# A selective scan on one core: all sixteen diagonals of B by way of DRAM, one state a transfer, and both parts of the step made by ScalarE

## The reference

```python
x_dbl = einsum('bkdl,kcd->bkcl', xs, x_proj_w)      # 40 rows: 8 of dt, 16 of B, 16 of C
delta = softplus(einsum('bkrl,kdr->bkdl', dts, dt_proj_w) + dt_proj_b)
def step(h, inp):                                   # h: (b, k, d, n)
    dA = exp(dt[..., None] * A4)
    h = dA * h + (dt * ut)[..., None] * bt[:, :, None, :]
    y = einsum('bkdn,bkn->bkd', h, ct)
```

## Time and profile before

| | |
|---|---|
| median of 3 runs | 6563.44 us (6556.88 to 6565.86) |
| profiled execution | 6549.5 us, span 6547.8 us |
| TensorE busy | 5769.2 us (88%) |
| VectorE busy | 4636.9 us (71%) |
| ScalarE busy | 3051.9 us (47%) |
| GpSimd busy | 2737.6 us (42%) |
| mean granted TensorE clock | 0.953 |
| DMA | 858.30 MB, mean 131 GB/s |

### The profile page before, as it was taken

The page is one execution under the profiler, slowest core; times in us unless marked ns, Lnnn a source line. Parts: engine busy times, 40 slices in busy tenths (PEclk is TensorE's granted clock), DMA queues, the critical chain, the costliest instruction groups (busy, mean ns, idle before and its releaser), DMA issues. The chain is left out here.

```text
span 6547.8 us, 128900 instructions
## 1 busy us (share of the span) xinstructions
PE 5769.2 (88%) x41691; PEld 5133.7 (78%) x41691; DVE 4636.9 (71%) x6690; ACT 3051.9 (47%) x5802; POOL 2737.6 (42%) x1648
## 2 busy tenths in 40 slices
PE   7799999999778999999997527999999979999998
PEld 5688888888657888888885415888888878888887
DVE  2799999999618999999995653556555565555554
ACT  2688888888537887888884211111111111111110
POOL 1688898889518898988893000000000000000000
PEclk8899999999889999999998868999999989999999
DMA  2455555554414555554542135666666666667665
GB/s 92 108 136 137 135 138 134 137 136 136 124 58 121 135 137 133 140 133 131 136 135 88 32 82 144 146 149 154 151 151 138 147 163 145 142 145 149 152 150 142
DMA packets 1081548, 858.30 MB, mean 131 GB/s; under 512 B 304598, under 2 KB 987446, under 8 KB 1046966
## 3 DMA queue, kind: packets, MB, share of 16 engines
q1 hardware_dynamic: 1080566, 844.65, 52.5%
q10 hardware_dynamic: 720, 10.49, 0.4%
HBM read 811.44 MB, written 43.55 MB: 131 GB/s over the span
## 5 line engine op out<-in xcount | busy, mean ns | idle before, releaser
L714 POOL TENSOR_TENSOR read<-state,c_wide 128x1024 f32<-128x1024 f32 x1024 | 2420.4, 2380 | 367.6 <-DVE state L763 361.3
L763 DVE TENSOR_TENSOR_SCAN state<-decay,carry,p_drive 128x512 f32<-128x512 f32 x1792 | 2152.8, 1260 | 53.8 <-POOL carry L718 24.8
L648 ACT ACTIVATE decay<-step,a_neg 128x512 f32<-128x512 f32 x2048 | 1422.2, 717 | 419.4 <-DVE state L763 405.3
L1646 PE MATMUL p_y<-window,x_high 128*128 128x256 f32 x7936 | 1497.4, 286 | 0.0
L1709 ACT COPY term_blocks<-p_s 128x256 f32<-128x256 f32 x832 | 310.4, 373 | 2184.8 <-PE p_s L1646 2184.8
L1646 PEld LDWEIGHTS p_y<-window,x_high 128*128 128x128 f32 x7936 | 1246.1, 191 | 0.0
L1646 PE MATMUL p_y<-window,x_low 128*128 128x256 f32 x3968 | 1134.2, 286 | 0.0
L542 PE MATMUL p_drive<-diag_b,xu_tok 128*128 128x128 f32 x8192 | 1068.4, 284 | 50.1 <-DVE state L763 50.1
L542 PEld LDWEIGHTS p_drive<-diag_b,xu_tok 128*128 128x128 f32 x8192 | 1006.2, 199 | 112.8 <-DVE state L763 107.8
L553 PE MATMUL p_y<-ident,read 128*128 128x128 f32 x8192 | 1077.6, 275 | 9.0 <-POOL read L714 5.9
L553 PEld LDWEIGHTS p_y<-ident,read 128*128 128x128 f32 x8192 | 940.1, 143 | 11.1 <-POOL read L714 11.1
(11 more groups left out here) (245 smaller groups left out, 5358.6 us busy)
## 6 DMA issues: line engine op xcount, KB each, us to landing
c_wide<-c_scratch SPq DMA_DIRECT2D x256, 1024.0 KB, 4.7
diag_b<-diag_scratch SPq DMA_DIRECT2D x256, 512.0 KB, 4.1
window<-taps_scratch SPq DMA_DIRECT2D x448, 257.0 KB, 6.3
window<-taps_scratch SPq DMA_DIRECT2D x768, 129.0 KB, 4.6
window<-taps_scratch SPq DMA_DIRECT2D x192, 513.0 KB, 7.2
window<-taps_scratch SPq DMA_DIRECT2D x64, 385.0 KB, 6.1
gate_scratch<-gate_out SPq DMA_DIRECT2D x16, 512.0 KB, 3.1
gate_in<-gate_scratch SPq DMA_DIRECT2D x8, 1024.0 KB, 6.4
```

Of the source, the lines that this page charges most:

```text
L648: act.activation(decay[:, n % 2, t, :], step[:, c.parity, t, :], ACT.Exp, scale=m.a_neg[:, DT2 * c.k + t, n:n + 1]).then_inc(s["decay"], 1)
L714: pool.tensor_tensor(read[:, n % 4, :, :], state[:, n % 4, :, :], wide, ALU.mult).then_inc(s["read_out"], 1)
L763: dve.tensor_tensor_scan(flip(state[:, n % 4, t, :], c), flip(decay[:, n % 2, t, :], c), flip(p_drive[:, n % 2, t, :], c), 0.0 if c.start ...
L1646: last = pe.matmul(out, x[:, source, blk, :], view[:, :, at:at + P][:, :, ::-1], start=first and x is m.x_high and z == 0, stop=True, skip ...
```

## The change

In the scan:

- every state's diagonal goes by way of DRAM: `store_rows` writes 16 x 512 single values where it wrote 8 x 512, `load_diag` loads one state (256 KB) a transfer into one of four slots, and `drive` is a product for every n. `turn_b`, `keep_b` and `times_b` are gone;
- both step products of a chunk stand at n = 2, in two banks (`p_prep` and `p_b`), and ScalarE makes both parts of the step from them (`step_parts`: |z| and max(z, 0) for each half), then one exponential of 1024 columns and one logarithm. `step_bias` of VectorE is gone;
- `turn_y`, `keep_y`, `add_y` and `keep_x` stand at other n;
- at the start 8 MB of zeros are written, where 4 MB were.

In the spectral layer the window `w` is loaded and waited for in two halves (`w` for slot 16, `v` for slot 18), and `build` is cut into `sum_weights` and `scale_weights` at slots 3 to 6. The attention frees its semaphores and ends with a barrier of all engines.

```diff
             def load_diag(c, n):
-                if not (c.first and d < 2):
-                    sp.wait_ge(s["driven"], START + c.q * 2 + (8 * d - 8))
-                at = 2 * d * NB4 * P * P
-                src = m.diag_dram[c.parity, at:at + 2 * NB4 * P * P].rearrange("(n p q) -> p n q", n=2 * NB4, p=P)
+                if not (c.first and n < 4):
+                    sp.wait_ge(s["driven"], START + c.q * 2 + (2 * n - 6))
+                src = m.diag_dram[c.parity, n * NB4 * P * P:(n + 1) * NB4 * P * P]
...
-                    ap=[[NB4 * P * P, ODD], [P * P, NB4], [P + 1, P]])
-                rows = xd[B_ROW + 1:B_ROW + NS:2, :].rearrange("n (i p) -> n i p", p=P)
+                    ap=[[NB4 * P * P, NS], [P * P, NB4], [P + 1, P]])
+                rows = xd[B_ROW:B_ROW + NS, :].rearrange("n (i p) -> n i p", p=P)
...
             def drive(c, n):
-                if n % 2 == 0:
-                    pe.wait_ge(s["scaled"], START + c.g * ODD + (n // 2 + 1))
-                elif n % 4 == 1:
-                    pe.wait_ge(s[f"diag_in{n // 4 % 2}"], START + c.g * 32 + (16 * (n // 8) + 16))
+                if n == 0:
+                    pe.wait_ge(s["x_kept"], START + c.g * 2 + 2)
+                pe.wait_ge(s[f"diag_in{n % 4}"], START + c.g * 64 + (16 * (n // 4) + 16))
...
-                        if n % 2 == 0:
-                            last = pe.transpose(o, scaled[:, i, t * P:t * P + P], m.ident[:, :])
-                        else:
-                            last = pe.matmul(o, xu_tok[:, c.parity, i, t * P:t * P + P],
-                                             diag[:, n // 4 % 2, n // 2 % 2, i, :], start=True, stop=True)
+                        last = pe.matmul(o, xu_tok[:, c.parity, i, t * P:t * P + P], diag[:, n % 4, i, :],
+                                         start=True, stop=True)
...
+            def step_parts(c):
+                if not c.first:
+                    act.wait_ge(s["decay"], START + c.q * 2 + -2 * NS)
+                act.wait_ge(s["x_turned"], START + c.g * 2)
+                for t in range(DT2):
+                    act.wait_ge(s["step_mm"], START + c.g * 2 + (t + 1))
+                    bias = m.dt_b[:, DT2 * c.k + t:DT2 * c.k + t + 1]
+                    bank = (p_prep, p_b)[t]
+                    act.activation(softplus[:, t, :], bank[:, :], ACT.Abs, bias=bias).then_inc(s["step_abs"], 1)
+                    act.activation(step[:, c.parity, t, :], bank[:, :], ACT.Relu, bias=bias).then_inc(s["step_max"], 1)
...
                 if c.first:
-                    step_bias(c, 0)
-                    step_bias(c, 1)
                     begin_y(0)
                     finish_step(c)
                     begin_y(1)
                 for n in range(NS):
                     scan(c, n, 0)
-                    if n in (6, 7) and not c.first:
-                        add_y(Before(c), n - 6)
-                    if nxt and n in (4, 5):
-                        step_bias(nxt, n - 4)
+                    if n in (7, 9) and not c.first:
+                        add_y(Before(c), n // 2 - 3)
                     if nxt and n == 8:
                         finish_step(nxt)
                     scan(c, n, 1)
...
-    "w": [(1, 256, 256), (1, 512, 512), (5, 128, 512)],
+    "w": [(1, 256, 256), (5, 128, 256)],
+    "v": [(1, 512, 512), (5, 384, 512)],
...
-                        build(n, k, 0)
+                    if i in (3, 5):
+                        sum_weights(n, k, (i - 3) // 2)
+                    if i in (4, 6):
+                        scale_weights(n, k, (i - 4) // 2)
```

More of the change, by code:

```diff
@@ L93, in _ @@
             sp.wait_ge(idmade, 4)
-            for parity in range(2):
-                sp.dma_start(m.diag_dram[parity].rearrange("(r x) -> r x", r=P), blank[:, :]).then_inc(m.w_stored, 16)
+            for part in range(4):
+                half = m.diag_dram[part // 2].rearrange("(h r x) -> h r x", h=2, r=P)[part % 2]
+                sp.dma_start(half, blank[:, :]).then_inc(m.w_stored, 16)
             sp.wait_ge(copied, 14)
@@ L407, in scans @@
         xd = sb("xd", [P, L])
-        b_tok = sb("b_tok", [P, 2, NB4, NS])
         c_wide = sb("c_wide", [P, 2, 4, L])
@@ L561, in turn_y @@
                     pe.wait_ge(s["y_kept"], START + c.g + 1)
-                    pe.wait_ge(s["b_kept"], START + c.g + (1 if c.last else 2))
+                    pe.wait_ge(s["step_max"], START + c.g * 2 + (2 if c.last else 6 if c.following else 4))
                 else:
@@ L571, in body @@
                     project(c)
-                    turn_b(c)
                     step_product(c, 0)
@@ L579, in body @@
                 for n in range(NS):
-                    if not c.first and n in (5, 6):
-                        turn_y(Before(c), n - 5)
+                    if not c.first and n in (6, 7):
+                        turn_y(Before(c), n - 6)
                     if nxt:
@@ L630, in step_ln @@
                 act.activation(softplus[:, :, :], softplus[:, :, :], ACT.Ln, bias=1.0).then_inc(s["step_ln"], 1)
-            def times_b(c, n):
-                if n == 0:
-                    act.wait_ge(s["b_kept"], START + c.g + 1)
-                    act.wait_ge(s["x_kept"], START + c.g * 2 + 2)
-                if not (c.first and n < 2):
-                    act.wait_ge(s["driven"], START + c.q * 2 + (2 * n - 2))
-                for i in range(NB4):
-                    last = act.activation(scaled[:, i, :], xu_tok[:, c.parity, i, :], ACT.Copy,
-                                          scale=b_tok[:, c.parity, i, n:n + 1])
-                last.then_inc(s["scaled"], 1)
             def decays(c, n, t):
@@ L669, in body @@
                     keep_projection(c)
-                    keep_b(c)
+                    step_parts(c)
                     step_exp(c)
@@ L674, in body @@
                     keep_x(c, 1)
-                    times_b(c, 0)
                     for n in range(2):
@@ L678, in body @@
                         decays(c, n, 1)
-                    times_b(c, 2)
                 for n in range(NS):
@@ L683, in body @@
                         decays(of, at, 0)
-                    of, at = following(c, nxt, n + 3)
-                    if of and at % 2 == 0:
-                        times_b(of, at)
                     of, at = following(c, nxt, n + 2)
@@ L689, in body @@
                         decays(of, at, 1)
-                    if n == 3 and not c.first:
+                    if n == 2 and not c.first:
                         keep_y(Before(c))
@@ L807, in __init__ @@
         self.g, self.q, self.first = c.g + -1, c.q + -NS, False
+        self.last, self.following = False, not c.last
         self.last = False
@@ L1174, in _ @@
                                                  ALU.mult, ALU.add).then_inc(s["res"], 1)
+    nc.clear_and_free_semaphores(list(s.values()))
+    nc.all_engine_barrier()
 KF, LAGS, FRACS = 16, 3, 4
@@ L1218, in held_in @@
         return "c"
-    return {0: "near", 1: "w", 3: "x" if g < 8 else "y"}[v]
+    return {0: "near", 1: "w" if g % 2 == 0 else "v", 3: "x" if g < 8 else "y"}[v]
 def columns(name, vector, lag):
-    at = 0
+    at = BEGIN.get(name, 0)
     for v, low, top in RUNS[name]:
@@ L1618, in body @@
                 load("w", k)
+                load("v", k)
                 if following is None:
@@ L1659, in slot @@
                 for j, (v, lag, blk) in enumerate(full):
-                    if i == 16 and v == 1:
-                        pe.wait_ge(s["in_w"], START + n * (32 * len(RUNS["w"])) + 32 * len(RUNS["w"]))
+                    if i in (16, 18) and v == 1:
+                        half = "w" if i == 16 else "v"
+                        pe.wait_ge(s["in_" + half], START + n * 64 + 64)
                     last = product(shared_bank(i), source, DIFF + blk // 2, held_in(g, v), v, lag, j == 0)
```

106 lines of the change are left out of this document (45 added, 61 removed).

## The result

The changed kernel takes 7029.46 us (median of 4 runs, 7019.83 to 7035.25) against 6560.16 us of the kernel before beside it: ratio 1.0714, interval 1.0697 to 1.0731. It is slower, as forecast, but by 469 us where the forecast had 263.

A forecast was written before the change was run, and what follows sets the result against it. VectorE leads before, TensorE after: 48.0 + 3.3 wait + 0.7 clock = 52.0 us a chunk, + 4.85 x 62 = + 301; with - 21 - 22 + 5, + 263 on 6549.5, as median 6826 us; range 6600 to 7050.

The forecast's parts named there:

- The mechanism: Scan: TensorE becomes the bound with 48.0 us of work a chunk and waits before drive 8 for diagonals behind the store.
- VectorE's relief: Scan: VectorE loses 2.9 us a chunk, down to 40.9, worth nothing because TensorE becomes the bound.
- The forecast proper: Whole kernel: waits of 1.5 to 5 us a chunk give 6696 to 6950 us; chance 0.61.
- rival B: Scan: store worse than linear, or clock falling in every chunk; 7167 us, milder half from 6950; chance 0.14.
- The wait: Scan: TensorE waits 3.3 us a chunk before drive 8 for its diagonal, load 8, queued behind the store.
- The store itself: Scan: 8192 single values in SyncE's one queue take 11.5 us, bounds 10 and 16, ending at T + 15.1.
- T: Scan: the end of drive 3, when load 7 and the store may go; TensorE wants drive 8 at T + 13.85.
- with the slower transfers behind a store and the landing T + 17.1: Scan: load 8 ends at T + 15.9, and with slow transfers and landing is there at T + 17.1.
- The clock term: Scan: waits go on provoking half clock on TensorE, taken as 0.7 us a chunk; 1.7 if in every chunk.
- In this regime scans have 3 us of slack: Scan: with TensorE the bound, scans have 3 us to the drive two states later, so VectorE no longer delays TensorE.
- case A: Scan: TensorE bounds but loads are in time, wait 0 to 1.5 us; 6590 to 6696 us; chance 0.17.
- The small terms: Outside the chunk: first chunk of each image -21 us, spectral rounds -22, zeros and barrier at the start + 5.

The follow-up runs named there:

- split_blocks_dve: split_blocks with VectorE making both parts of the step again, as in step_on_dve; 6775.87 us, ratio 1.0323 to the kernel before.
- keep_busy: The changed kernel with 40 transposes of the identity put ahead of drive 8 in each chunk; 6910.34 us, ratio 1.0555 to the kernel before.
- half_rows: The changed kernel storing only the diagonals of states 0 to 7, 4096 values in place of 8192; 6741.06 us, ratio 1.0299 to the kernel before.
- store_act: The changed kernel with both stores issued by ScalarE in its own queue, not SyncE's; 6803.02 us, ratio 1.0395 to the kernel before.
- split_blocks: The changed kernel with the store cut into four between the loads, each 128 places of all sixteen rows; 6726.64 us, ratio 1.0275 to the kernel before.
- step_on_dve: The changed kernel with VectorE making both step parts again and ScalarE's exponential in two halves; 6870.99 us, ratio 1.0496 to the kernel before.
- adjacent_rows: The kernel before, storing the adjacent rows 0 to 7 of B in place of the odd ones; 6567.92 us, ratio 1.0004.

## Why the prediction was right, and where its sizes were off

**The mechanism was right.** TensorE is the bound; it waits once a chunk, before drive 8, for the diagonals behind the store; and the sign follows. VectorE's relief was said to be worth nothing, and that is nearly so: by split_blocks_dve it is worth 31 us (by the ratios) to 49 us (by the medians), while in the changed kernel itself undoing it even wins 158 us. The drive costs 1.79 us for each state (842.42 to 844.21), as forecast, and TensorE's work is 48.8 us by keep_busy against 48.0. half_rows, store_act and split_blocks each take most or all of the wait away in another way and win 226 to 303 us.

**The place in the range owes something to luck.** The forecast proper, waits of 1.5 to 5 us, ended at 6950 us. The measured 7029 us lie above it, in what the range took in of rival B ("the clock falls in every chunk", chance 0.14), 20 us short of the range's end at 7050. That half of B is what happened: the wait stayed under 5 us, and the clock falls behind it in 61 of the 62 chunks that have a store, where the kernel before has it in 32 of 62 (low stretches of the granted clock, counted in the traces).

**The wait was undersized: 4.55 us a chunk, not 3.3.** The store itself was oversized: issued at 832.61, 1.15 us behind the end of drive 3 at T = 831.46, its values are nearly through by 844, T + 12.5, where the working had T + 15.1. But the transfers behind it are slow for six microseconds, where the working allowed about one: load 8 is there at T + 18.8 in place of T + 17.1. Two errors, 2.6 us too much and 4.3 too little, met in one sum, so that the wait came out only 1.3 us short. The working also had SyncE issue load 8 as soon as its slot was free, while that issue is held until 843.3, when the store is nearly through. (One end of the bounds was added up wrongly: a store of 10 us gives T + 3.6 + 10 + 0.8 = T + 14.4 and a wait of 0.5, not 14.1 and 0.3.) The earlier trace rows had shown the slow transfers; the step "with the slower transfers behind a store and the landing T + 17.1" took too little for them.

**The clock term was undersized most: 2.26 us a chunk, not 0.7.** The forecast left half of the falls out, since before the falls came in half of the chunks. With TensorE waiting 4.55 us at the same place in every chunk the clock falls each time, and in the window it is at half for 64.9 us, 5.1 a chunk, where the working had 3.4 for a fall. The Trainium skill ("TensorE: Matmul & The Clock Gate", section "HAM oscillation — how this bites in real kernels") says that a recurring DMA wait in a loop throttles the clock in each pass; the trace agrees, with the 61 of 62 chunks. The 1.7 us that the prediction had for a fall in every chunk was the better number, and still too low.

**VectorE is closer behind than the forecast had it.** "In this regime scans have 3 us of slack" holds in the changed kernel only because TensorE stands still for the diagonals. Where that is gone, in split_blocks, TensorE waits for the scans 17.2 / 13.9 = 1.2 us a chunk by its products alone, up to 3.1 with its weight loads (25.6 + 17.2), and the chunk is 50.22 us. So case A's 6590 to 6696 could not have been reached with the loads in time: the runs put it at 6727. In the changed kernel itself these waits are 0.5 us a chunk, and some 0.2 us remain that the sum had not.

The chunk is then 48.0 + 4.55 + 2.26 + 0.7 = 55.5 us, as measured. The scan of the two images, from the first scan to the last, is longer by 533 us (62 x 8.38 = 520, and 14 in the first and last chunks) where the forecast had 301.

**The small terms were right.** The first image's first scan starts at 210.2 us in place of 222.5, and the second's comes 9.9 us sooner after the last of the first image, together 22.2, as forecast (-21): `begin_y` starts at 181.69 and the step is ready at 193.3. SyncE's wait for the lone store grows from 7.1 to 13.6 us; the forecast had 6 more. What follows the last scan is 25.5 us shorter (-22 forecast for the spectral layer): in 1000 us TensorE's wait for the window, 22.2 us in 13 waits before, is gone, and that for the joins has grown from 12.5 us in 11 waits to 21.3 in 26. That is 1.6 us a round, where the working had 3.6. The extra zeros cost nothing (the projection starts at 181.84 us, at 181.89 in the earlier trace rows), where the sum had 5. In all 533.4 - 22.2 - 25.5 = + 485.7, the difference of the two profiled spans (7033.5 - 6547.8).

**What each part is worth**, by the runs: all states by products and through DRAM cost TensorE some 7 us of work a chunk, which leaves even the best arrangement tried, split_blocks, 2.8% behind the kernel before. The store adds 5.3 us a chunk to that (55.53 - 50.22), 303 us by the medians. The step on ScalarE is worth 136 us where VectorE leads, 31 to 49 where TensorE leads and the loads are in time, and costs 158 us in the changed kernel; the spectral part is worth 26 us in the kernel before and about as much in the changed one.

**Open.** Why the store and what follows it end sooner when the step is on VectorE (step_on_dve, 14.2 us to landing) or when TensorE is kept busy (keep_busy, 14.6) than in the changed kernel (16.5). split_blocks_dve shows that step_on_dve's gain needs the store's wait; what in ScalarE's passes or in the time of the issue lengthens the store was not tried apart. Why the loads behind the store are slow, and whether SyncE's held issue is a cause of that or only goes with it, was not tried either. Nor were the new places of `turn_y`, `keep_y`, `add_y` and `keep_x` tried apart from the rest.

## What to carry to other kernels

When a change moves work to the engine that is nearly the bound, first add up that engine's whole loop: here 41.2 + 7 us on TensorE decided the sign, whatever VectorE gave back. A transfer of single values cost twice in its queue here: its own time, and the slow transfers behind it. Look at what stands right behind it and when that is wanted, look at how long the issues behind it take, and try parts that draw from many partitions. And when an engine stalls for some microseconds at the same place in each pass, price the clock's fall behind the stall too: here it was half as much again (2.26 on 4.55 us).

## What the runs showed of the hardware

- The length of a store of single values depends on the partitions that it reads, and not on its number of values alone. From the first value until 98% have begun, the median of the stores between 300 and 1500 us: 4096 values in 5.0 us from eight rows in every second partition and 6.4 us from eight adjacent ones (adjacent_rows; 7.6 in half_rows). 8192 values in 9.8 us from sixteen adjacent rows (8.8 and 8.9 in keep_busy and step_on_dve), 8.3 us from sixteen in every second partition. 2048 values in 6.5 us from four adjacent rows, 1.6 us from all sixteen, where the places written differ too.
- Behind the store shown, loads ran at 65 to 104 GB/s for six microseconds and then at 366 GB/s.
- SyncE's issue of the load behind such a store took 6.7 to 10.4 us in 13 chunks of the changed kernel, where 0.36 us is the median.
- An elementwise product of 128 x 1024 on GpSimd took 10.95 us beside a long instruction of VectorE with two tensor operands (193.41 us, first chunk; 10.90 in the kernel before), against 2.37 us in the other chunks:

```profile
193.41 10.95 POOL L685 TENSOR_TENSOR shared<-step,s 128x1024 f32<-128x1024 f32 x1 [13.44 <-DVE step L720]
```
